# Attention heads in a decoder kernel: the softmax shifted by one head against the normalisation, the value-output product in three rounded parts

## What is computed

```python
x = _rmsnorm(hidden_states, ln_weight)
h_q = (x @ w_q.T).reshape(b, lq, H, DH)
h_k = (key_value_states @ w_k.T).reshape(b, lk, H, DH)
h_v = (key_value_states @ w_v.T).reshape(b, lk, H, DH)
score = jnp.einsum('bqhd,bkhd->bhqk', h_q, h_k) + position_bias[None]
score = jnp.where(m, score, -jnp.inf)
score = jax.nn.softmax(score, axis=-1)
score = jnp.where(m, score, 0.0)
attn = jnp.einsum('bhqk,bkhd->bqhd', score, h_v).reshape(b, lq, H * DH)
out = attn @ w_out.T
```

## Time and profile before

| | |
|---|---|
| median of 3 runs | 782.0 us (781.49 to 782.08) |
| the profiled execution | 782.88 us, of which its span is 781.1 us |
| instructions in the span | 12357 |
| TensorE, matmuls | 738.4 us busy, 95% |
| VectorE | 486.3 us, 62% |
| ScalarE | 402.5 us, 52% |
| POOL | 91.6 us, 12% |

### The profile page before, as it was taken

One profiled execution on the slowest core, in us unless ns is written; L12 is line 12 of the kernel. 1 busy time (PEld: TensorE's weight loads), 2 busy tenths in 40 slices (PEclk: granted clock), 3 DMA queues, 4 the chain that ended last, 5 costly groups with the idle time before them and its releaser, 6 DMA issues.

```text
span 781.1 us, 12357 instructions
## 1 busy us (share of the span) xinstructions
PE 738.4 (95%) x4320; PEld 582.0 (75%) x4320; DVE 486.3 (62%) x823; ACT 402.5 (52%) x617; POOL 91.6 (12%) x86
## 2 busy tenths in 40 slices
PE   6999999999988999999999999999999878998994
PEld 4888888888867777777777777777777547886883
DVE  5653467534352688777886586665566647578655
ACT  5433333333345666655676666766666444554452
POOL 2010000090017000000000031000000001304503
PEclk9999999999999999999999999999999999999998
DMA  9353241332625788888886777766765323542641
GB/s 331 117 219 136 84 145 54 108 122 81 241 83 179 247 300 288 265 272 290 278 277 210 227 240 232 226 222 225 245 220 175 106 96 110 155 141 84 214 133 54
DMA packets 60039, 145.09 MB, mean 186 GB/s; under 512 B 6752, under 2 KB 6768, under 8 KB 59344
## 3 DMA queue, kind: packets, MB, share of 16 engines
q1 hardware_dynamic: 58400, 136.73, 53.8%
q0 software_dynamic: 1360, 7.23, 2.4%
q10 hardware_dynamic: 224, 0.39, 0.2%
HBM read 142.23 MB, written 2.10 MB: 185 GB/s over the span
## 4 chain that ended last, share of the span: by engine, by line
PE 82%; DVE 11%; issue 2%; ACT 2%; DMA 2%; POOL 1%; DVEq 0%; ACTq 0%; POOLq 0%
PE bank L468 25%; PE acc L468 16%; PE bank L640 7%; PE bank L586 7%; PE acc L721 7%; PE bank L699 6%; PE bank L682 5%; PE bank L605 5%; DVE score L1319 2%; DVE prob L1347 1%; DVE row_sum L1341 1%; DVE piece_top L1335 1%; DVE neg_max L1325 1%; PE bank L500 1%; PE bank L666 1%
## 5 line engine op out<-in xcount | busy, mean ns | idle before, releaser
L468 PE MATMUL bank<-feat_hi,a_hi 128*128 128x512 f32 x352 | 139.3, 396 | 11.0 <-DVE feat_lo L1102 7.5
L468 PE MATMUL bank<-feat_lo,a_hi 128*128 128x512 f32 x352 | 138.0, 392 | 0.0
L1102 DVE TENSOR_TENSOR a_lo<-a_raw,a_hi 128x1024 fp32r<-128x1024 f32 (+1 forms) x45 | 55.4, 1232 | 124.3 <-ACT a_hi L867 118.0
L996 ACT ACTIVATE t_ring<-bank 128x512 f32<-128x512 f32 x64 | 70.1, 1095 | 86.3 <-PE bank L605 86.3
L586 PEld LDWEIGHTS bank<-few_ctx,ak 128*128 128x128 f32 x512 | 62.8, 193 | 45.1 <-issue 42.4
L468 PE MATMUL acc<-b_hi,tile_hi 128*128 128x512 f32 x224 | 87.7, 392 | 3.6 <-issue 1.9
L1341 DVE TENSOR_REDUCE row_sum<-prob 128x4 f32<-128x512 f32 x64 | 43.7, 683 | 71.3 <-ACT prob L1011 70.9
L468 PEld LDWEIGHTS bank<-feat_hi,a_hi 128*128 128x128 f32 x352 | 66.8, 190 | 28.0 <-DVE a_lo L1102 9.6
L468 PE MATMUL acc<-b_hi,tile_lo 128*128 128x512 f32 x224 | 87.2, 389 | 0.0
L605 PEld LDWEIGHTS bank<-k_ring,wq 128*128 128x128 f32 x512 | 64.5, 192 | 18.7 <-issue 13.4
L586 PE MATMUL bank<-few_ctx,ak 128*128 128x128 f32 x512 | 74.4, 289 | 3.4 <-DMA ak<-ax 2.1
(11 more groups left out here) (113 smaller groups left out, 1097.4 us busy)
## 6 DMA issues: line engine op xcount, KB each, us to landing
ak<-ax SPq DMA_DIRECT2D x64, 512.0 KB, 3.8
wq<-wqn SPq DMA_DIRECT2D x64, 256.0 KB, 4.2
wv<-wvh SPq DMA_DIRECT2D x64, 256.0 KB, 3.4
wo<-bx SPq DMA_DIRECT2D x64, 256.0 KB, 4.0
a_raw<-w SPq DMA_DIRECT2D x22, 512.0 KB, 4.1
a_raw<-a SPq DMA_DIRECT2D x21, 512.0 KB, 3.7
b_raw<-b SPq DMA_DIRECT2D x34, 256.0 KB, 2.7
pair<-w SPq DMA_DIRECT2D x24, 352.0 KB, 4.4
```

What stands on the lines that cost most here:

```text
L468: mm = pe.matmul(out_ap, w, x, start=start and k == 0, stop=stop and k == len(products) - 1, skip_group_check=True)
L996: act.activation(t_ring[n // GH % 2][:].rearrange("p c b k h -> p (c b k h)")[:, n % GH:GH * N:GH], bank[0][:], ACT.Copy).then_inc(t_ok, 1)
L1102: return dve.tensor_tensor(out_ap, whole, high, ALU.subtract)
```

## The change

Three things change together.

1. `outer` becomes three rounded products in the way `few`. ScalarE rounds `wo` (`round_wo`), POOL takes the rest (`wo_rest`), VectorE rounds the values and takes their rest (`split_values`).
2. On ScalarE and VectorE the softmax runs one head ahead: iteration n holds the maximum and shift of head n+1 ahead of the normalisation of head n, and the exponentials of head n+1 at the end of ScalarE's iteration. VectorE's `divide` moves from head n-1 to head n.
3. TensorE's second half of the scores (`group_scores(g+1, 1)`) moves in the fourth head of a group from behind `outer` to the place between `weigh` and `keys`. POOL's normalisations are cut into steps between its `wo_rest`.

```diff
+        wo_hi, wo_lo = tile_hi, tile_lo
+        v_hi, v_lo = [b_hi[i][:, 0:P] for i in range(2)], [b_lo[i][:, 0:P] for i in range(2)]
...
                 if n >= 2:
                     sp.wait_ge(out_used, n - 1)
+                    sp.wait_ge(wo_lo_ok, n - 1)
                 sp.dma_start(wo[n % 2][:], bx[n % HEADS]).then_inc(wo_dma[n % 2], 16)
...
+            def wo_rest(n):
+
+                pool.wait_ge(wo_hi_ok, n + 1)
+                pool.tensor_tensor(wo_lo[n % 2][:], wo[n % 2][:], wo_hi[n % 2][:].bitcast(F32),
+                                   ALU.subtract).then_inc(wo_lo_ok, 1)
...
-            normalise(1)
...
+            scales(1)
+            for n in range(HN):
+                if n < TT:
+                    centre(1, n)
+                elif n < 2 * TT:
+                    level(1, n - TT)
+                wo_rest(n)
...
                     if few:
-                        pe.wait_ge(wo_dma[par], 16 * (n // 2 + 1))
-                        mm = pe.matmul(bank[1][:], v_sb[par][:, 0:P], wo[par][:], start=True, stop=True)
+                        pe.wait_ge(v_lo_ok, n + 1)
+                        pe.wait_ge(wo_lo_ok, n + 1)
+                        mm = passes(bank[1][:], v_hi[par], v_lo[par], wo_hi[par][:], wo_lo[par][:], True, True)
...
+                    if few and j == 3 and n >= -1 and g + 1 < HALVES * GROUPS:
+                        group_scores(g + 1, 1)
...
-                    if few and j >= 2 and g + 1 < HALVES * GROUPS and n >= -2:
-                        group_scores(g + 1, j - 2)
+                    if few and j == 2 and g + 1 < HALVES * GROUPS and n >= -2:
+                        group_scores(g + 1, 0)
...
+            def round_wo(n):
+
+                act.wait_ge(wo_dma[n % 2], 16 * (n // 2 + 1))
+                if n >= 2:
+                    act.wait_ge(u_mm, n - 1)
+                    act.wait_ge(wo_lo_ok, n - 1)
+                else:
+                    act.wait_ge(b_used, T30)
+                act.activation(wo_hi[n % 2][:], wo[n % 2][:], ACT.Copy).then_inc(wo_hi_ok, 1)
...
                 if n >= 1:
                     copy_turned(n - 1)
-                if n >= 0:
-                    exponentials(n)
+                    round_wo(n - 1)
...
                 if n >= 1:
                     copy_outer(n - 1)
+                if 0 <= n + 1 < HN:
+                    exponentials(n + 1)
...
+            def split_values(n):
+
+                dve.wait_ge(v_ok, n + 1)
...
+                dve.tensor_copy(v_hi[n % 2], v_sb[n % 2][:, 0:P]).then_inc(v_hi_ok, 1)
+                dve.wait_ge(v_hi_ok, n + 1)
+                low(v_lo[n % 2], v_sb[n % 2][:, 0:P], v_hi[n % 2].bitcast(F32)).then_inc(v_lo_ok, 1)
...
             for n in range(-LEAD_K, HN):
+                m = n + 1
+                if 0 <= m < HN:
+                    if m % GH == 0:
+                        add_mask(m)
+                    find_max(m)
                 if n >= 1:
-                    divide(n - 1)
+                    split_values(n - 1)
                 if n >= 0:
-                    if n % GH == 0:
-                        add_mask(n)
-                    find_max(n)
-                    if n % GH == 0:
-                        add_mask(n + 1)
-                    if n % GH == 1:
-                        add_mask(n + 1)
-                        add_mask(n + 2)
+                    divide(n)
+                if 0 <= m < HN:
+                    if m % GH == 0:
+                        add_mask(m + 1)
+                    if m % GH == 1:
+                        add_mask(m + 1)
+                        add_mask(m + 2)
```

More of the change, by code:

```diff
@@ L396, in scales, with centre, level @@
                 ins.then_inc(scale_ok, 1)
+            def centre(p, t):
+                if t == 0:
+                    pool.wait_ge(scale_ok, p + 1)
+                x = resid[:, (p % 2) * TT + t, :]
+                pool.tensor_scalar(x, x, moments[:, t, 0:1], scale[:, t:t + 1], ALU.subtract,
+                                   ALU.mult).then_inc(normed_ok if p < 2 else operand_ok if p < 4 else part_ok, 1)
+            def level(p, t):
+                pool.wait_ge(normed_ok, p * TT + t + 1)
+                pool.tensor_scalar(normed[:, t, :], resid[:, (p % 2) * TT + t, :], rms_scale[:, t:t + 1], None,
+                                   ALU.mult).then_inc(operand_ok, 1)
             def normalise(p):
                 scales(p)
-                pool.wait_ge(scale_ok, p + 1)
                 for t in range(TT):
-                    x = resid[:, (p % 2) * TT + t, :]
-                    ins = pool.tensor_scalar(x, x, moments[:, t, 0:1], scale[:, t:t + 1], ALU.subtract, ALU.mult)
-                    ins.then_inc(normed_ok if p < 2 else operand_ok if p < 4 else part_ok, 1)
+                    centre(p, t)
                 if p < 2:
                     for t in range(TT):
-                        pool.wait_ge(normed_ok, p * TT + t + 1)
-                        pool.tensor_scalar(normed[:, t, :], resid[:, (p % 2) * TT + t, :], rms_scale[:, t:t + 1], None,
-                                           ALU.mult).then_inc(operand_ok, 1)
+                        level(p, t)
+            def wo_rest(n):
+                pool.wait_ge(wo_hi_ok, n + 1)
+                pool.tensor_tensor(wo_lo[n % 2][:], wo[n % 2][:], wo_hi[n % 2][:].bitcast(F32),
+                                   ALU.subtract).then_inc(wo_lo_ok, 1)
             load_stage(1, xT[1])
@@ L430, in _ @@
             pool.wait_ge(xn_ok, C)
-            normalise(1)
[L433 to L437, removed]
+            scales(1)
[5 more added lines that the diff above has]
+                wo_rest(n)
+                if n == GH + SCANS + 2:
+                    pool.wait_ge(top_ok, 1)
+                    pool.partition_all_reduce(piece_all[:, 1:2], piece_all[:, 0:1], P, bass.bass_isa.ReduceOp.max).then_inc(all_ok, 1)
+                    pool.wait_ge(all_ok, 1)
+                    pool.tensor_copy(low_flag[:], piece_all[:, 1:2]).then_inc(flag_ok, 1)
+                if n == HEADS + 4:
+                    scales(2)
+                if HEADS + 4 < n <= HEADS + 4 + TT:
+                    centre(2, n - HEADS - 5)
             def add_scaled(p, t):
@@ L1054, in step3 @@
                      f + (s0 + h * F3), last_block=True, f=f, split_next=split_next)
+            round_wo(HN - 1)
             silu(A30, s0, True, 0)
@@ L1059, in _ @@
             split_a(A30 + 1, (A30 + 1) % 2)
+            act.wait_ge(wo_lo_ok, HN)
+            act.wait_ge(v_lo_ok, HN)
             split_b(T30, T30 % 2)
@@ L1388, in step3 @@
                      f + (s0 + h * F3), last_block=True, f=f, split_next=split_next, after=after)
-            divide(HN - 1)
+            split_values(HN - 1)
             split_a(A30 + 1, (A30 + 1) % 2)
```

6 lines of the change are left out of this document (added).

## The result

The changed kernel takes 839.87 us (median of 6 runs, 838.89 to 842.28), the kernel before 782.16 in the runs beside it: a ratio of 1.0736 [1.0714, 1.0757], 7.4% slower. The forecast was 828, from 802 to 852, slower with 0.88. The profiled execution took 841.7 us with a span of 839.9, against the span of 781.1 before: 58.8 us to find.

What follows compares the result with a forecast made beforehand. TensorE alone was taken to bound ordinary heads. Six scan groups x 4.6 = 27.6, nine others x 2.77 = 24.9, last about even, less 3 for waits and 3 for first heads: +46, so 828 us, range 802 to 852.

Steps and rivals of the forecast that it cites:

- an ordinary head: Heads j = 0 to 2 of a group: `outer` waits for POOL's rest until 4.70; head 5.48 against 4.99.
- the last head of a group: Head j = 3: `outer` waits for VectorE's split of the values until 6.99; head 7.67, 0.89 dearer.
- the scan groups: Heads 4 to 27, six groups: VectorE's work comes late, each group 4.6 dearer, 27.6 in all.
- The 12 us for the scan's mask: Scan heads: POOL might also stretch VectorE's one-input mask, some 0.5 in up to 24 heads; up to 12 us, outside the sum.
- the outer's slot: Outer product on TensorE: three rounded products take 0.68 instead of 0.93, 0.25 less a head, 16 us in all.
- POOL beside VectorE: VectorE's two-input operations meeting POOL grow by about 0.6, POOL by 0.2 to 0.4; three heads cost 1.88 more than now.
- Loads and POOL's steps: Weight loads and POOL's centring stay hidden: `wo` with 1.4 to spare, centring of 2.1 each done before 3.3 of the next head.
- the last group: The final group of heads, with neither queries nor later scores, would come out about even.
- The 3 us for the first heads: First heads: 3 us less, since the exponential's table load is no longer in the way.
- Faster: Rival: rests ready before `outer` asks, TensorE stays the bound, 762 us; decided by POOL's duration, under 0.82 for no loss; chance 0.10.
- The queue of loads: Rival: in scan heads later loads expose `wo`, 0.5 to 1 a head, 12 to 24 us, 845 to 855; chance 0.11.
- The clock: Rival: TensorE's short waits bring the granted clock to 0.83 in the attention, about 870 us; chance 0.03.

Runs made afterwards that it cites:

- e4_early: The changed kernel with raw weights in three buffers, loaded and rounded one head earlier: 812.01 us.
- e11_behind_weigh: The changed kernel with the second half of the scores between `weigh` and `keys`, instead of between queries and transpose: 842.58 us.
- e3_split: The changed kernel with the values' split ahead of the next head's mask, maximum and shift on VectorE: 824.12 us.
- e6_all: The changed kernel with the values' split first, weights rounded a head earlier in three buffers, and VectorE taking the rests of heads 31 to 33: 797.76 us.
- e12_dve_rests: As e6_all, but VectorE takes every rest of the weights and POOL none: 786.54 us.
- e2_reduce: The changed kernel with VectorE, not POOL, taking the weights' rests of heads 31 to 33, around the reduction: 830.53 us.
- e8_one_input: As e6_all, but POOL multiplies one tile by 0.0 instead of subtracting two, so the third partial product is left out of the result: 785.61 us.
- e9_no_move: The kernel before with softmax one head ahead, full float32 outer product, second half of the scores left behind `outer`: 843.06 us, ratio 1.0800.

## Why the prediction was right, and where it was off

**Right: an ordinary head.** 4.70 for the rest, 5.48 for the head; the trace has 4.66 (4.59 and the handover of 0.07) and 5.50. The query copy was placed at 1.22 and stood at 1.22, the rounding's end at 3.25 in both. The last 0.02 owes something to offset: POOL took 0.05 less than its term and the slot 0.09 more. The 0.10 for the first weight load had no row; from the rest to the outer the trace has 0.07. Every link was an in-order queue with its duration in a row, and `e4_early` shows that this wait goes when the chain begins a head earlier.

**Right: the last head of a group.** 7.67 predicted, 7.49 measured, but by two errors that offset each other: the scores stand earlier, so the mask starts at 2.89 and not at 4.16, and the shift, which then falls on POOL's rest, takes 1.67 and not 0.69. `e11_behind_weigh`, with the place that I had assumed, gave 7.89, and its shift took 0.69: there the chain was right term by term, to 0.2.

**Right: the scan groups.** 27.6 predicted, 25.6 measured, of which each group is 4.3 and not 4.6. (Before the change such a group takes 24.9 by the transposes, not the 24 of the text.) The 12 us for the scan's mask, kept out of the sum, would have been too much: in the changed kernel the mask (L1389) had a longest duration of 0.524. That isn't because POOL leaves it alone. None of its 24 ran beside a rest of POOL; in `e3_split` two did, and took 1.59.

**Mis-sized: the outer's slot.** The term was 3 x 0.226 = 0.68; it measured 0.77, and the same with no wait (599.45 to 600.22 in `e4_early`, whose POOL was done before). In the rows of the first block such products follow each other; here the first of the three costs 0.31 to the next, the others 0.23 (599.45, 599.76, 599.99, 600.22). The gain is 10 us and not 16, as `e4_early`, with no wait left in ordinary heads, shows.

**Mis-sized: POOL beside VectorE.** I took 0.6 more for an operation that meets POOL, though the earlier trace rows themselves have 1.48 - 0.69 = 0.79 and 2.30 - 1.23 = 1.07. The shift measured 0.98 more, the scaling up to 1.1, and a product of four columns went from 0.16 to 1.28. The sum stood up since few of these meetings are on the path in the changed kernel: over the span they come to some 47 us of VectorE's time (mean less median of its 64: 18.6 in the shift, 11.0 in the copy of the values, 4.1 in their rest, 10.6 in the four-column product, 2.7 in the scaling). In `e6_all`, once the waits are gone, they weigh more: 11 us, the distance to `e12_dve_rests`.

**Missed: the reduction.** The step "*Loads and POOL's steps*" named centring alone on POOL's queue and called it hidden. `partition_all_reduce` and its two gaps were moved between two rests as well, and before the change nobody waited behind them. One distance of 16.64, where the one at this place of a group is 5.49 elsewhere, is 11.1 us, nearly all of the 12 between 828 and 840: a wait of 10.2 where 0.5 is usual, and 1.4 for work at the lower clock. `e2_reduce` took 9.3 of it back. The diff shown with the change left these lines out, and so did I.

**The sum.** Predicted +46: 27.6 in the scan groups, 18.9 everywhere else. Measured +58.8: 25.6 in the scan groups, 11.1 for the reduction, and 22.1 for the rest of the table. Of these, 5.2 are in the last heads, where I had called the last group about even. The 3 us for the first heads didn't come: the first transpose is 2.3 earlier, but the first group 3.5 longer. A group behind the reduction is 2.3 dearer and not 2.77. That total and place agree this well is in part luck: the missed 11 us are outside it, and some of these misses offset each other.

**The rivals.** "Faster" hung on POOL's duration by my text. `e4_early` reached the 4.83 head with POOL at 1.27, so the condition was stated too narrowly: an earlier start does the same. It still isn't faster than before, as `e6_all` shows. The queue of loads: TensorE's waits list no `wo` load in the attention, and the rounding waited for it five times, 3.5 us in all and 1.4 at the longest. Three of these loads, under the scan, are on the chain that ended last, so the 1.4 to spare were gone now and then, as that rival had it, but not for its 12 to 24 us. The clock: 1.00 from 500 to 650 us, with a wait of 0.5 us in head after head. It fell at the stall, and for 4 us each at 313 and 682; by busy time and granted clock in steps of 1 us I estimate 6 us for the three. The rule on HAM oscillation (the Trainium skill, TensorE: Matmul & The Clock Gate, A second HAM failure mode), that frequent short idling of TensorE makes the clock oscillate, did not come true for the waits of 0.5 us.

## What to carry to other kernels

An engine that is idle is free only if nothing it touches is shared: price a helper by what it does to its neighbour, and try the neighbour doing the work itself. When work is given to such an engine, go through everything else in its queue, rare instructions above all, since each now stands in front of a product. And when edits come together, run the order of the work and the arithmetic apart: here one was a gain of 0.7% and the other hid it.

## What the runs showed of the hardware that I had not expected

**POOL's rest and VectorE's shift exclude each other, and the one that starts first goes through.** In the changed kernel 20 shifts started behind a rest of POOL, by 0.13 to 0.57 us. Every one ended 0.54 to 0.56 after POOL's end, whenever it had started, as at 588.39 (POOL's end 589.52, the shift's 590.06); the scaling in `e6_all` likewise (540.94, 542.20, 542.75). Twelve shifts started first. They took their 0.69, and POOL's operation, 1.27 when alone, took up to 1.78 and ended 1.12 to 1.27 after them. A product of 128x4 and a copy of 128x128 wait just as long:

```profile
L1401 DVE TENSOR_TENSOR row_inv<-row_inv,row_valid x64: 161/162/1278, 249.7 to 688.9; 128x4 f32<-128x4 f32 x64
```

```profile
L1382 DVE CAST b_hi<-v_sb x64: 212/220/1297, 253.0 to 693.4; 128x128 fp32r<-128x128 f32 x64
```

Not all of VectorE's operations are caught. In `e6_all` 20 row sums and maxima, with one input in SBUF and four columns out, started behind POOL's start and all took 0.68. The copy has a single input in SBUF and is caught, and so is the scan's mask, in `e3_split`:

```profile
L1389 DVE TENSOR_SCALAR pair<-pair x24: 509/517/1592, 275.6 to 441.0; 128x704 int32<-128x704 int32 x24
```

The Trainium skill (GPSIMD Engine Reference, Key points) names both forms, two SBUF inputs and a 2-port mode, as contending; the rows agree for the first. For the copy and the mask they agree as far as these run in such a mode, which no row shows.

**With one input POOL holds VectorE for less of its time.** In `e8_one_input` the shifts that started up to 0.45 behind POOL ended 0.33 to 0.37 before POOL's end, not 0.54 after it; those that started 0.57 or more behind took their 0.69.

**POOL pays twice around a reduction across partitions**: 6.40 before it and 7.56 after, with no instruction to be seen (6.30 before it in `e2_reduce`). The Trainium skill (GPSIMD Engine Reference, Instruction dispatch) has about 6 us for the first call to freshly loaded code, with no visible instruction; the gap before the reduction agrees, and the gap behind it is longer.

**The granted clock fell behind waits of very different length, and not behind the shortest.** With 0.5 us in each head it stayed at 1.00 from 500 to 650 us. It fell to the 1.2 GHz level in the stall of 10 us; from 313 to 317 us, behind two heads with waits of 1.55 and 2.15; and eight times in `e9_no_move`, with a wait of about 3 in each group.
